# The first feed-forward layer in a two-layer transformer kernel goes from 32-bit planes with turns by TensorE to scaled 16-bit planes with turns by DMA

## The reference, cut to what matters

```python
x = x + quantised_matmul(layernorm(x), ctx)                 # first part, called l0 in the kernel
x = x + ffn0(layernorm(x), W, b, A, B, router_W, router_b)  # the layer that is changed
x = x + attention(layernorm(x), ctx, ctx, mask, wq, wk, wv, wo)  # 32 query heads, 8 key/value heads
x = x + ffn1(layernorm(x), ...)

def ffn0(x, W, b, A, B, router_W, router_b):
    q = x[:, 179:-1, :].mean(axis=1)                # mean over 332 rows of the batch
    routing = softmax(q @ router_W.T + router_b)    # 8 experts, per batch
    base = x @ W.T + b                              # 1024 x 1024
    t = einsum('bsd,erd->bser', x, A)               # rank 16 for each expert
    return base + 2 * einsum('bser,eor,be->bso', t, B, routing)
```

## Time and profile before

| | us |
|---|---|
| median of 3 runs | 1977.05 |
| lowest and highest | 1975.38, 1977.3 |
| the profiled execution | 1974.47 |
| its span in the profile | 1972.7 |

### The profile page before, as it was taken

How to read it: one execution, slowest core, us unless ns; L and a number is a source line. 1 busy time by engine, 2 the same in 40 slices (tenths; PEclk the granted TensorE clock), 3 DMA queues, 4 the chain that set the end, 5 groups by cost and what they waited for, 6 DMA issues and landing times.

```text
span 1972.7 us, 25980 instructions
## 1 busy us (share of the span) xinstructions
PE 1937.5 (98%) x9044; PEld 1055.8 (54%) x9044; DVE 1561.9 (79%) x2687; ACT 1113.1 (56%) x1765; POOL 1238.7 (63%) x753
## 2 busy tenths in 40 slices
PE   8999999999989999999999999999999999999999
PEld 6886786878734444444444444444444444444444
DVE  5877778587588888999888888878989998878563
...
GB/s 255 193 202 124 180 237 227 164 160 208 295 194 208 190 168 153 192 192 183 197 146 183 167 198 212 189 218 210 162 166 170 184 177 179 155 208 143 186 53 76
DMA packets 701809, 360.16 MB, mean 183 GB/s; under 512 B 602000, under 2 KB 629008, under 8 KB 701680
## 3 DMA queue, kind: packets, MB, share of 16 engines
...
HBM read 180.17 MB, written 29.36 MB: 106 GB/s over the span
## 4 chain that ended last, share of the span: by engine, by line
PE 79%; DVE 5%; DMA 2%; ACT 2%; issue 1%; POOL 1%; SPq 1%; ACTq 0%; DVEq 0%; POOLq 0%
PE ps L43 26%; PE ps L45 26%; PE ps L44 26%; PE ps L960 1%; DMA x_lo<-x_scratch 1%; POOL u_sb L2331 1%; DMA pT<-pp 1%; DVE psb L1778 1%; DMA raw<-in_ctxT 0%; PE ps L967 0%; DVE t_sb L1323 0%; DVE t_sb L1321 0%; SPq L722 0%; DVE u_sb L1320 0%; DVE ta L1308 0%
## 5 line engine op out<-in xcount | busy, mean ns | idle before, releaser
L1793 DVE SCALAR_TENSOR_TENSOR pp<-psb,st,pp 128x1024 f16<-128x1024 f32 x256 | 369.1, 1442 | 40.9 <-ACT pp L2210 38.8
L1778 DVE CUSTOM_DVE_ANT_0 psb<-ps,mask,sc 128x1024 f32<-128x1024 f32 x256 | 327.1, 1278 | 89.6 <-PE ps L45 88.6
L2210 ACT ACTIVATE pp<-psb,st 128x1024 f16<-128x1024 f32 x256 | 293.1, 1145 | 180.5 <-DVE st L1788 171.2
L2203 ACT ACTIVATE psb<-psb,st 128x1024 f32<-128x1024 f32 x256 | 293.6, 1147 | 91.9 <-DVE st L1778 91.7
L2374 POOL TENSOR_SCALAR araw<-araw,kst 128x512 f32<-128x512 f32 x128 | 290.7, 2272 | 42.0 <-DMA araw<-in_wq 42.0
L2374 POOL TENSOR_SCALAR araw<-araw,sc 128x512 f32<-128x512 f32 x128 | 216.1, 1688 | 14.0 <-DMA araw<-in_wo 14.0
L2387 POOL TENSOR_TENSOR ua<-ua,ta 128x512 f32<-128x512 f32 x64 | 143.1, 2236 | 115.0 <-DVE ta L1308 114.9
L2379 POOL TENSOR_TENSOR wol<-araw,woh 128x512 f16<-128x512 f32 x128 | 153.5, 1199 | 89.4 <-ACT woh L2149 89.3
L1807 DVE SCALAR_TENSOR_TENSOR x_lo<-ps,sc,x_lo 128x512 f32<-128x512 f32 x256 | 191.5, 748 | 19.5 <-PE ps L45 12.7
L43 PE MATMUL ps<-pT,vsb 128*128 128x512 f16 x512 | 195.0, 381 | 4.5 <-DMA pT<-pp 4.5
L43 PE MATMUL ps<-woh,osb 128*128 128x512 f16 x512 | 194.1, 379 | 4.3 <-DVE x_lo L1807 4.2
...
## 6 DMA issues: line engine op xcount, KB each, us to landing
araw<-in_wq SPq DMA_DIRECT2D x128, 256.0 KB, 3.6
araw<-in_wo SPq DMA_DIRECT2D x128, 256.0 KB, 3.4
scan<-in_wq SPq DMA_DIRECT2D x64, 256.0 KB, 4.7
scan<-in_wo SPq DMA_DIRECT2D x64, 256.0 KB, 4.8
raw<-in_wv SPq DMA_DIRECT2D x16, 512.0 KB, 5.0
raw<-in_ctxT SPq DMA_DIRECT2D x16, 512.0 KB, 4.6
raw<-in_wk SPq DMA_DIRECT2D x16, 512.0 KB, 5.7
raw<-in_ctx SPq DMA_DIRECT2D x16, 512.0 KB, 4.6
```

Source lines behind the costliest of these rows:

```text
L1778: e.tensor_tensor_reduce(out=psb[:, n % 3, :], in0=pair(n % 2 * 2), in1=mask[:, i, :], scale=sc[:, 23 - H // 32:24 - H // 32], scalar=-LOW ...
L1793: e.scalar_tensor_tensor(out=pp[:, r, 1024:2048], in0=psb[:, r, :], scalar=st[:, n // 4 % 4, 16 + i:17 + i], in1=pp[:, r, 0:1024], op0=ALU ...
L2203: e.activation(P, P, ACT.Exp, bias=c[:, i:i + 1], scale=-1.0, accum_out=c[:, 8 + i:9 + i]).then_inc(a_exp.sem, 1)
L2210: e.activation(pp[:, r, 0:1024], psb[:, r, :], ACT.Copy, scale=st[:, n // 4 % 4, 16 + i:17 + i]).then_inc(a_ph.sem, 1)
```

## The change

The layer's products go to 16-bit planes. Its weight slices and `loraA` are scaled by powers of two while they are split; for that the sums of squares of `W` and `loraA` are taken in the steps (18 pieces more, `square`), reduced at step 42 by `ffn_squares` on TensorE, and made into factors at step 44 by `ffn_scale` on VectorE. `loraB` and the planes of the low-rank result stay 32-bit. The tiles are normalised with a scale of 1024, and `ffn_add` and the router take the scales out again.

A tile is now split before it is turned: `ffn_hi` and `ffn_lo` read the normalised tile from SBUF and write 16-bit planes `fp` (128 x 2048), and one DMA transpose on SP (`turn_f`) writes both planes, turned, to `h2f`. For attention's rows of batch 0, `h_hi` and `h_lo` write `hp`, and `turn_h` issues four DMA transposes of 128 x 512 per tile, straight into `hTa`, `hTb`, `hTc`. The store and the load of `h_scratch` for batch 0 are gone. TensorE's twelve turns of this stage are gone. The slices `c17`, `c18`, `c19` are loaded and split in steps 53 to 60, tiles 0 to 3 are split at steps 55, 57, 59 and 63, and the queues of SP, TensorE, VectorE and ScalarE in the layer's stage are in a new order. `row_sums` reads both planes in one instruction. Buffers lie in other places (`qsb`, `hTa`, `hTb`, `h4t01`, `up_ha`, `up_hb` among them), and the banks of PSUM for tiles 3 to 7 are others.

```diff
-TEMP.update({("f", i): (0, 1, 2, 0, 2, 0, 4, 3)[i] for i in range(8)})
-TEMP.update({("h", i): (1, 2, 4, 3)[i] for i in range(4)})
-TEMP.update({("r", 0): 1, ("r", 1): 0})
+TEMP.update({("f", i): i % 2 for i in range(8)})
+TEMP.update({("h", i): i % 2 for i in range(4)})
+TEMP.update({("r", 0): 2, ("r", 1): 2})
...
-FFN_BANKS = [[0, 1], [2, 6], [3, 4]] + [[0, 1], [2, 3]] * 2 + [[0, 1]]
+FFN_BANKS = [[0, 1], [2, 6], [3, 4], [0, 1], [2, 6], [3, 4], [0, 1], [5, 2]]
...
+                      + [*range(39, 47)] * 2 + [47] + [*range(10, 18), 47] + [*range(39, 48)])
+SQUARE_LOAD_STEP = [max(SQUARE_STEPS[n - 7] + 1 if n > 6 else 0, SQUARE_STEPS[n] - 2) for n in range(99)]
+SQUARES = range(163)
...
-    h2s = alloc(h2, "h2s", [128, 4, 2, 8, 128], F32R)
+    h2f = alloc(h2, "h2f", [128, 4, 16, 128], F16)
+    w18 = alloc(h2, "w18", [128, 2, 2, 1024], F16)
+    fp = alloc(h2, "fp", [128, 2, 2048], F16)
...
-        return h2s[:, :, hl, k, :]
+        return h2f[:, :, 8 * hl + k, :]
...
+    def w_plane(n, hl):
+
+        if n in (18, 19):
+            return w18[:, n - 18, hl, :]
+        if n < 22:
+            return w16[:, n - 16 if n < 18 else n - 18, hl, :]
+        return w22[:, hl, :] if n == 22 else sink[:, :].bitcast(F16)[:, hl * 1024:hl * 1024 + 1024]
...
-    FFN_TURN_AT = {56: 0, 58: 1}
+    W_SPLIT_AT = {50: "c16", 54: "c17", 58: "c18", 60: "c19"}
+    FFN_LOW_AT = {55: 0, 57: 1, 59: 2, 63: 3}
...
+        def turn_f(tile):
+            e.wait_ge(v_h2.sem, v_h2[tile])
+            if tile > 3:
+                e.wait_ge(t_fm.sem, t_fm[tile - 4, 1])
+                e.wait_ge(t_lt.sem, t_lt[0])
+                e.wait_ge(v_rt.sem, v_rt[0, 0])
...
+            if s in FFN_LOW_AT and s < 63:
+                turn_f(FFN_LOW_AT[s])
+        load_raw("w32")
+        turn_f(3)
         store(63)
-        for key in ("c22", "c23", "w32", "w33"):
-            load_raw(key)
+        load_raw("w33")
 
...
+        def turn_h(tile):
+            e.wait_ge(v_klo.sem, v_klo["h", tile])
+            for w in range(4):
+                if tile:
+                    e.wait_ge(d_h[w].sem, d_h[w]["h", tile - 1])
+                e.dma_start_transpose(hT_part(w)[:, tile, :, :, :].rearrange("p l k t -> p (l k) t"),
+                                      hp[:, tile % 2, w, :, :].rearrange("p l c -> p (l c)")).then_inc(d_h[w].sem, 16)
...
+        load_squares(0, 7)
         e.wait_ge(t_kv.sem, t_kv[63])
         weights_split(e)
         for n in range(4):
             load_w(("q", n))
-        for n in range(88, 130):
-            load_square(n)
-        for i in range(4):
-            store_h(i)
-            for n in (range(130, 136), range(136, 141), range(141, 145), [])[i]:
-                load_square(n)
-            if i == 1:
-                store_x2(4)
-                store_x2(5)
-
-
-        e.wait_ge(t_lt.sem, t_lt[1])
-        e.wait_ge(t_fm.sem, t_fm[5, 1])
-        load_h(0, 0)
-        load_h(0, 1)
-
-        for i in (4, 5):
-            e.wait_ge(d_x[i].sem, d_x[i]["store"])
-        load_h(0, 2)
-        e.wait_ge(t_htr.sem, t_htr["h", 3])
-        load_h(0, 3)
-        for n in range(4, 6):
-            load_w(("q", n))
-        e.dma_start(cosq[:, :], A["cosq"]).then_inc(d_tab.sem, 16)
-        e.dma_start(sinq[:, :], A["sinq"]).then_inc(d_tab.sem, 16)
-        store_x2(6)
-
-        e.wait_ge(t_fl.sem, t_fl.last)
+        load_squares(7, 11)
+        turn_f(4)
+        load_squares(11, 17)
+        turn_f(5)
+        load_squares(17, 26)
+        turn_f(6)
+        load_squares(26, 35)
+        turn_f(7)
+        load_squares(35, 40)
+        e.wait_ge(v_kr.sem, v_kr[63])
+        turn_h(0)
+        load_squares(40, 45)
+        turn_h(1)
+        load_squares(45, 47)
+        turn_h(2)
+        load_squares(47, 54)
+        turn_h(3)
         for o in range(2):
             e.wait_ge(d_khl[o].sem, d_khl[o][62 + o])
             e.wait_ge(d_vhl[o].sem, d_vhl[o].last)
         load_k(0)
-        for i in range(3):
-            load_mask(0, i)
+        load_mask(0, 0)
+        load_mask(0, 1)
+        load_squares(54, 64)
+        for i in (4, 5):
+            store_x2(i)
+        for n in range(4, 6):
+            load_w(("q", n))
+        for i in (4, 5):
+            e.wait_ge(d_x[i].sem, d_x[i]["store"])
+        e.dma_start(cosq[:, :], A["cosq"]).then_inc(d_tab.sem, 16)
+        e.dma_start(sinq[:, :], A["sinq"]).then_inc(d_tab.sem, 16)
+        load_mask(0, 2)
+        load_mask(0, 3)
+        store_x2(6)
         load_w(("q", 6))
-        load_mask(0, 3)
+        e.wait_ge(t_fl.sem, t_fl.last)
+        load_w(("q", 7))
         load_v(0)
         store_x2(7)
-        load_w(("q", 7))
...
+        def ffn_squares():
+            e.wait_ge(a_sq.sem, a_sq[17])
+            e.wait_ge(v_kc.sem, v_kc["c1", 0])
+            e.matmul(ps[:, 4, 0:18], twos[:, :], squares[:, 146:164], start=True, stop=True).then_inc(t_kc.sem, 1)
...
-        def turn_tile(key, bk):
-            e.wait_ge(v_h.sem, v_h[key])
-            for j in range(8):
-                m = e.transpose(ps[:, bk + j // 4, j % 4 * 128:j % 4 * 128 + 128], temp(key)[:, j * 128:j * 128 + 128],
-                                identf[:, :])
-            m.then_inc(t_htr.sem, 1)
...
+            m = mm3(e, bank(bk), h2f[:, i, k, :], h2f[:, i, 8 + k, :], w_plane(16 + k, 0)[:, nh * 512:nh * 512 + 512],
+                    w_plane(16 + k, 1)[:, nh * 512:nh * 512 + 512], k == 0, False)
...
-        e.wait_ge(v_h2.sem, v_h2[1])
+        for r in range(2):
+            e.wait_ge(d_f[r].sem, d_f[r][r])
...
-            if k in (2, 6):
-                ffn_turn(2 + k // 6)
...
+        lora_t(0)
         ffn_half(2, 0)
         router_end(0)
-        lora_t(0)
         ffn_half(2, 1)
         ffn_end(0)
         ffn_end(1)
         ffn_end(2)
         ffn_half(3, 0)
-        ffn_turn(4)
         ffn_half(3, 1)
-        ffn_turn(5)
         ffn_half(4, 0)
         ffn_end(3)
-        ffn_turn(6)
         ffn_half(4, 1)
-        ffn_turn(7)
         ffn_half(5, 0)
-        h_turn(0)
+        ffn_half(5, 1)
+        ffn_half(6, 0)
         lora_t(1)
         router_end(1)
-        ffn_half(5, 1)
-        h_turn(1)
+        ffn_half(6, 1)
         ffn_end(4)
         ffn_end(5)
-        ffn_half(6, 0)
-        h_turn(2)
-        ffn_half(6, 1)
-        h_turn(3)
         ffn_end(6)
         ffn_half(7, 0)
...
+                e.scalar_tensor_tensor(out=split_dst(key, 1), in0=raw_at(key), scalar=fsc[:, 11:12] if key == "w32" else fsc[:, 10:11],
+                                       in1=split_dst(key, 0), op0=ALU.mult, op1=ALU.subtract).then_inc(v_lo.sem, 1)
+                return
...
+            planes = fp[:, tile % 2, :]
+            tt(planes[:, 1024:2048], temp(("f", tile)), planes[:, 0:1024], ALU.subtract).then_inc(v_h2.sem, 1)
...
+            e.wait_ge(d_f[tile % 2].sem, d_f[tile % 2][tile])
...
+            m = e.tensor_reduce(c[:, 0:16], h2f[:, i, :, rows], AX, ALU.add)
...
+            planes = hp[:, tile % 2, :, :, :]
+            tt(planes[:, :, 1, :], temp(("h", tile)).rearrange("p (w c) -> p w c", w=4), planes[:, :, 0, :],
+               ALU.subtract).then_inc(v_klo.sem, 1)
...
-        split_lo("c19")
         split_lo("c20")
         split_lo("c21")
-        ffn_lo(2)
+        ffn_norm(4)
+        split_lo("c22")
+        split_lo("c23")
         query_sums()
-        split_lo("c22")
+        split_lo("w32")
+        ffn_lo(4)
         row_sums(1)
-        split_lo("c23")
-        split_lo("w32")
-        ffn_lo(3)
         row_sums(2)
         router(0)
         split_lo("w33")
-        ffn_norm(4)
+        ffn_norm(5)
         router_end(0)
+        lora_scale(0)
+        ffn_lo(5)
         query_scale()
         value_squares()
-        ffn_norm(5)
-        lora_scale(0)
         ffn_add(0)
         ffn_add(1)
+        ffn_norm(6)
         ffn_add(2)
-        ffn_lo(4)
-        ffn_norm(6)
-        ffn_lo(5)
+        ffn_lo(6)
+        ffn_norm(7)
+        h_norm(0)
+        ffn_lo(7)
+        h_norm(1)
+        h_lo(0)
         row_sums(5)
         ffn_add(3)
-        ffn_norm(7)
-        ffn_lo(6)
+        h_norm(2)
+        h_lo(1)
         row_sums(6)
-        h_norm(0)
-        ffn_lo(7)
+        h_norm(3)
+        h_lo(2)
         router(1)
-        h_norm(1)
-        h_lo(0)
+        h_lo(3)
         router_end(1)
         lora_scale(1)
-        h_norm(2)
         ffn_add(4)
-        h_lo(1)
         ffn_add(5)
-        h_norm(3)
-        h_lo(2)
-        h_lo(3)
         ffn_add(6)
         ffn_add(7)
...
+        split_hi("c21")
+        root(("f", 4))
+        split_hi("c22")
+        split_hi("c23")
+        split_hi("w32")
         ffn_hi(4)
-        for n in range(89, 94):
-            square(n)
+        split_hi("w33")
+        output_squares(0, 4)
+        root(("f", 5))
+        router_exp(0)
+        lora_hi(0)
+        ffn_hi(5)
+        output_squares(4, 10)
         root(("f", 6))
-        for n in range(94, 97):
-            square(n)
```

(44 more changed lines are left out.)

354 lines of the change are left out of this document (188 added, 166 removed), and 2 rows, old and new, of the table RAW.

## The result

| | median us | runs |
|---|---|---|
| before | 1975.72 (1970.55 to 1979.01) | 20 |
| after | 1982.02 (1977.83 to 1988.53) | 20 |

The ratio is 1.0036, with a 95% interval of 1.0028 to 1.0044: 6.3 us slower, where 10.5 us faster was forecast. 16.8 us have to be found.

The account below looks back on a forecast made before the run. TensorE was taken to bound the layer and attention. 14.9 us less work, 2.5 given back and 1.9 lost in the tail save 10.5 us: 1966.5 us, range 1957 to 1975 us.

Parts of the forecast that it names:

- TensorE's work, -14.9 us: Mostly feed-forward layer: 16-bit products save 4.7 us, twelve removed turns 10.4, an added reduction costs 0.2.
- 2.5 us given back in the layer: Feed-forward layer: new TensorE waits on VectorE sum to 5.5 us against 3.0 us of gaps today.
- The wait at the second router product: Layer: `router(1)` ready at 493.0 us where TensorE arrives at 490.9, behind VectorE's normalisations and splits; 2.1 us.
- 15 us in stages where ScalarE is about half idle: nothing: Steps 10 to 17 and 39 to 47: 18 more squares at 0.8 us each on ScalarE and SP cost nothing.
- item (3) of the prediction: Step 42: the added reduction of 18 sums of squares on TensorE costs 0.2 us.
- Slices c16 to c19 are split before that: Ahead of the layer: these splits finish before VectorE ends the last key step, taken as 403.0 us.
- moved work of steps 55 to 59: Three `turn_f` on SP hold up weight loads that have two steps of 5.4 us in hand; cost nothing.
- The tail, 1.9 us (bounds 0 and 6): Behind the layer: rotation tables land about 525.5 us, `q_part(0)` done at 523.7; last square at 517 to 519.
- slow rival: `turn_h` issues take 3.0 us each, delaying squares, stores and tables; rotation 16 us later, 1993 us; chance 0.07.
- The load of the transfers: Layer's stage: DMA engines busy 100 us of the new 115 us, 87%; called full but sufficient.
- The signs that I named: Products 0.216 us apart, layer's end near 518 us, rotation near 526, waits at c22 and second router, `turn_h` issues 0.75 us.
- signs of being wrong: `turn_h` issues over 1.7 us, last square well after the layer's end, or a layer tile landing later than TensorE wants.

Follow-up runs that it names:

- e13: Changed kernel with the c19 load and split placed as in e5 and the tail as in e10, squares left in place; 1971.63 us, ratio 0.9982.
- e5: Changed kernel with c19's load moved to step 59, ahead of `turn_f(2)`, and its split moved from step 60 to 62; ratio 1.0017.
- e2: Changed kernel without the 18 added squares and their loads, constants standing for their sums, `ffn_scale` kept; ratio 1.0011.
- e12: Kernel before plus only the 18 extra squares and their loads, sums unused; 1980.85 against 1974.99 us, ratio 1.0028.
- e10: Changed kernel with x2 stores and last ten square loads ahead of first keys and masks, sum of squares behind first query's products; 1975.38 us, ratio 1.0007.
- e15: e13 with the 18 squares and their loads also left out, constants standing for their sums; 1966.71 us, ratio 0.9956.

## Why the prediction was wrong

- **TensorE's work, -14.9 us:** right. Products 0.216 us apart, no turns; the layer is 13.5 us shorter between its first and last product although 2.3 us of it are slow products, and two of the turns lay outside.
- **2.5 us given back in the layer:** right in kind. In the changed kernel the waits for slices were hidden by the layer's late start, and 1.5 us for `ts_sb` and 0.4 us for c23 came; with the door mended c20, c22 and c23 cost 2.2 to 3.1 us (e13, e5). The wait at the second router product never came.
- **"15 us in stages where ScalarE is about half idle: nothing":** the first step that failed. The term was mis-sized: 5.9 us measured, in the changed kernel (e2) and alone (e12). Half idle was true, but much of the idle time lies where ScalarE waits for GpSimd (3 to 5 us at a key, for its sum), and what is issued behind that wait stands in front of the root or the cast that VectorE needs next. How much of the 5.9 us are the loads is open.
- **The scale's own work, not in the sum:** item (3) of the prediction counts the reduction on TensorE, 0.2 us, and nothing for `ffn_scale`, which holds VectorE for 3.7 us at step 44. Without the squares the table is still 2.1 us late (e2). No run leaves `ffn_scale` out, so its part of the time is open.
- **"Slices c16 to c19 are split before that" and the moved work of steps 55 to 59 at nothing:** failed. I took VectorE to be done with the last key step 1.5 us before TensorE. It was in arrears through c19, whose load stood behind `turn_f(2)` on SP: TensorE stood 5.6 us at the door, and 4 us came back (e5). The prediction did list the three transposes that hold up loads in these steps, and gave them cover of two steps; c19's had none.
- **The tail, 1.9 us (bounds 0 and 6):** mis-sized. 8.9 us were lost up to the first scores, and 6 us came back with e10. A quarter of a transpose holds SP 1.27 us and not 0.75, so 16 take 20 us and not 12; and the last squares land late because the transfers are full from 491 us on. The prediction took the lateness to come through the tables; it came through the sum of squares. The slow rival named this mechanism (squares behind `turn_h`) and put its threshold at 1.7 us per issue, where the tail alone would use up the lead. The issues stayed below it. The tail cost 8.9 us of a lead of 10.5 even so, and with the two losses ahead of it, of the squares and at the door, the kernel became slower.
- **The clock behind a wait:** priced in the slow rival alone (2.5 us), at nothing in the sum. In the changed kernel it takes part in all three losses, 1.7, 2.3 and 2.5 us.
- **The load of the transfers:** 87% was forecast for the layer, 83.9% measured from 418 to 530 us; "full but sufficient" was true of its mean and false of the last 30 us, at 97%.
- **Sum:** 5.9 + 4 + 6 = 16 us of the 16.8 us between forecast and result (4.9 + 3.8 + 5.7 = 14.4 us by the ratios alone), and e15, with all three taken out at once, gives 15.8 us. It is at 1966.7 us, 8.1 us under the kernel before in the same comparison, where 10.5 was forecast. The 2.4 us that are left lie within its interval, so whether `ffn_scale` costs them stays open.
- **The signs that I named:** products' distance held; the layer's end (518) and the rotation (526) came at 529 and 545; issues of `turn_h` of 0.75 us and waits at c22 did not come in the changed kernel. Of the signs of being wrong one came: the last square ends 5.5 us behind the layer's last product (536.15 and 530.70 us).
